# A graph layer's edge pass on one core: its last 13 quads written out per engine, and two gathers of padding left out

## What is computed

```python
k, q, v = (typed_linear(x, ntype, W).reshape(n, H, HD) for W in (Wk, Wq, Wv))
kw = typed_linear_heads(k[src], etype, att)
a = jnp.sum(kw * q[dst], axis=-1) * pri[:, etype].T / np.float32(np.sqrt(HD))
amax = jax.ops.segment_max(a, dst, num_segments=n)
ae = jnp.exp(a - amax[dst])
w = ae / jax.ops.segment_sum(ae, dst, num_segments=n)[dst]
m = typed_linear_heads(v[src], etype, msg) * w[:, :, None]
h = jax.ops.segment_sum(m, dst, num_segments=n).reshape(n, D)
h = typed_linear(h, ntype, Wa)
return h * alpha + x * (1 - alpha)      # alpha = sigmoid(skip)[ntype]
```

## Time and profile before

| | |
|---|---|
| median of 3 runs | 6516.59 us |
| the profiled execution | 6516.66 us |
| its span in the profile | 6514.9 us |
| PE busy | 4628.8 us (71%) |
| DVE busy | 4972.8 us (76%) |
| ACT busy | 4070.1 us (62%) |
| POOL busy | 4223.8 us (65%) |
| longest line of POOL (L563) | 3965.9 us in 4095 gathers |

### The profile page before, as it was taken

The page is one execution under the profiler, slowest core; times in us unless marked ns, Lnnn a source line. Parts: engine busy times, 40 slices in busy tenths (PEclk is TensorE's granted clock), DMA queues, the critical chain, the costliest instruction groups (busy, mean ns, idle before and its releaser), DMA issues.

```text
span 6514.9 us, 170550 instructions
## 1 busy us (share of the span) xinstructions
PE 4628.8 (71%) x33358; PEld 3951.0 (61%) x33359; DVE 4972.8 (76%) x14638; ACT 4070.1 (62%) x10772; POOL 4223.8 (65%) x4629
## 2 busy tenths in 40 slices
PE   7766666696666666976666679766666786666665
PEld 6665555575565555765655567655665676555553
DVE  6777777787777777777777777777777778777776
ACT  3467666645666665456666654666666547666665
POOL 1577777526777774277777743777777347777773
PEclk9888888798888888988888879788888898888887
DMA  6433333353333333533333335333333353333331
GB/s 223 140 108 107 107 107 108 91 235 104 107 107 107 107 107 101 230 99 107 107 107 107 107 120 210 100 107 106 107 107 106 139 191 102 107 107 106 106 108 54
DMA packets 306187, 783.84 MB, mean 120 GB/s; under 512 B 105775, under 2 KB 138900, under 8 KB 305012
## 3 DMA queue, kind: packets, MB, share of 16 engines
q0 software_dynamic: 196560, 537.00, 28.8%
q1 hardware_dynamic: 109092, 241.62, 9.9%
HBM read 573.87 MB, written 195.88 MB: 118 GB/s over the span
## 4 chain that ended last, share of the span: by engine, by line
PE 29%; DVEq 21%; issue 18%; DVE 17%; POOL 7%; DMA 4%; ACT 2%; ACTq 1%; POOLq 0%; SPq 0%
POOL rows L563 7%; DVEq L1446 7%; DVEq L1436 6%; PE ps L701 5%; PE ps L879 4%; PE ps L863 4%; DMA rows<-table,idx_now 3%; PE ps L884 3%; PE ps L725 3%; DVEq L286 3%; PE ps L712 3%; PE ps L695 2%; DVE prod L1430 2%; PE ps L878 1%; DVE wmsg L1408 1%
## 5 line engine op out<-in xcount | busy, mean ns | idle before, releaser
L563 POOL DMA_INDIRECT rows<-table,idx_now x4095 | 3965.9, 968 | 1389.4 <-issue 1145.7
L998 ACT ACTIVATE prod<-iota_n,dloc 128x128 bf16<-128x128 f32 x6240 | 1983.6, 389 | 21.0 <-issue 1.8
L878 PE MATMUL ps<-zeros,identb 128*128 128x132 bf16 x2080 | 516.5, 248 | 1517.8 <-DVE wmsg L1408 1248.1
L863 PE MATMUL ps<-qn,ohT 128*128 x8320 | 1429.9, 325 | 81.3 <-issue 61.7
L863 PEld LDWEIGHTS ps<-qn,ohT 128*128 128x128 f32 x8320 | 1252.1, 230 | 161.6 <-issue 143.1
L878 PEld LDWEIGHTS ps<-zeros,identb 128*128 128x128 bf16 x2080 | 225.1, 108 | 1690.6 <-issue 1571.4
L1003 ACT ACTIVATE ohf<-prod,ones 128x512 f32<-128x512 bf16 x1040 | 750.7, 722 | 731.4 <-PE ps L884 652.2
L879 PE MATMUL ps<-wmsg,ohf 128*128 128x132 f32 x4160 | 1122.8, 359 | 0.0
L1404 DVE TENSOR_TENSOR wmsg<-rows,weight 128x512 f32<-128x512 f32 x1040 | 724.1, 696 | 341.0 <-issue 309.4
L884 PE MATMUL ps<-wmsg,ohf 128*128 128x132 f32 x4160 | 976.2, 323 | 0.0
L1430 DVE TENSOR_TENSOR prod<-ps,rows 128x512 f32<-128x512 f32 x1040 | 716.5, 689 | 270.8 <-DMA rows<-table,idx_now 134.7
(11 more groups left out here) (166 smaller groups left out, 5474.2 us busy)
## 6 DMA issues: line engine op xcount, KB each, us to landing
table<-rows SPq DMA_DIRECT2D x245, 768.0 KB, 3.3
stage<-table SPq DMA_DIRECT2D x8320, 1.0 KB
rows<-table,idx_now POOLq DMA_INDIRECT x4095
rows<-in_node_type SPq DMA_DIRECT2D x5, 2613.0 KB, 10.5
rows<-stage SPq DMA_DIRECT2D x65, 128.0 KB
rows<-in_node_type SPq DMA_DIRECT2D x5, 512.0 KB, 4.2
out<-h SPq DMA_DIRECT2D x3, 704.0 KB
idx_row<-row_of SPq DMA_DIRECT2D x65, 0.5 KB
```

The lines of the kernel that those rows point to most:

```text
L563: pool.indirect_dma_start(out=rows[:, slot, j, :], out_offset=None, in_=table, in_offset=bass.IndirectOffsetOnAxis(ap=idx_now[:, half, c:c ...
L863: last = pe.matmul(ps[:, 2 + b, j * P:(j + 1) * P], ohT[:, b, j, :], qn[:, at(ts[j]), :].rearrange("p a c -> p (a c)"), start=True, stop=True)
L878: pe.matmul(bank[:, AW:2 * AW], identb[:], zeros[:], start=True, stop=True)
L998: act.activation(squares[:, turn % 2, j * P:(j + 1) * P], iota_n[:], ACT.Square, bias=dloc[:, at(4 * q + j)], scale=-1.0)
```

## The change

It does four things:

1. **No padding gathers.** In slot 15 SP's rows are now those of step 0 and POOL gathers steps 1 to 3. In quad 207 POOL gathers step 1 alone (step 829), and the two padding steps keep old rows of the ring; their edges are masked as before. DVE's wait counts follow (`LAST_PLACE`, `landed`). That is 2 gathers less per layer, 4085 in all.
2. **The tail is a function of its own on PE, ACT and DVE**, called behind `positions`, which ends at quad 207. REST = 196 is the first quad that the tail sums, FINAL = 25 the last block.
3. **On PE** each of the first three pieces stands ahead of the sum that it stood behind, and piece 3 stands right behind piece 2, ahead of the sums of quads 198 and 199.
4. **On DVE** the add of quad 195 moves from ahead of piece 0 to behind it, the add of 196 from ahead of piece 1 to behind it, and the weigh of 198 and the add of 197 from ahead of piece 2 to behind it. ACT's order is unchanged.

```diff
+LAST_PLACE = 48 * (QUADS // 16 - 1) + 16 * (STEPS - 4 * (QUADS - 1) - 1)
...
-            for q in range(QUADS - RING, QUADS + LAG + 1):
+            for q in range(QUADS - RING, QUADS):
...
-                sp.dma_start(rows[:, RING - 1, 3, :], stage[:]).then_inc(s_side, 16)
+                sp.dma_start(rows[:, RING - 1, 0, :], stage[:]).then_inc(s_side, 16)
...
-                    for j in range(3 if slot == RING - 1 else 4):
+                    for j in (range(1, STEPS - 4 * (QUADS - 1)) if is_last(q, QUADS) else
+                              range(1, 4) if slot == RING - 1 else range(4)):
...
-                        ta = tiles_of(a, mybir.EngineType.PE)
...
-                        ...
...
+                        sum_group(a, b)
...
+                def tail():
+
+                    softmax_piece(0, FINAL, FINAL % 2)
+                    sum_group(REST, 0)
+                    softmax_piece(1, FINAL, FINAL % 2)
+                    sum_group(REST + 1, 1)
+                    softmax_piece(2, FINAL, FINAL % 2)
+                    softmax_piece(3, FINAL, FINAL % 2)
+                    for a in range(REST + 2, QUADS):
+                        sum_group(a, a % 2)
+
+                def sum_group(a, b):
+                    ta = tiles_of(a, mybir.EngineType.PE)
...
+                    ...
...
+                tail()
...
+                def exponents(m):
+                    act.wait_ge(s_smd, l * (SM * BLOCKS) + SM * m + 3)
+                    act.activation(fade4[:, 1, :], fade4[:, 0, :], ACT.Exp)
+                    act.activation(aT[:], aT[:], ACT.Exp).then_inc(s_sme, 1)
...
+                def tail():
+                    for a in range(REST + 1, QUADS):
+                        onehot(ohf, a, a % 2, a, l * QUADS + a - 1).then_inc(s_ohf, 1)
+                        if a == REST + 3:
+                            exponents(FINAL)
...
-                              idx[:].rearrange("p (n s) -> p n s", s=2 * BS)[:, :, 2 * BS - 1:2 * BS],
+                              idx[:].rearrange("p (n s) -> p n s", s=2 * BS)[:, :, 2 * BS - 4:2 * BS - 3],
...
-                            dve.wait_ge(s_gath[slot], (l * (QUADS // RING) + use) * 48 + 48)
+                            landed = 16 * (STEPS - 4 * (QUADS - 1) - 1) if is_last(q, QUADS) else 48
+                            dve.wait_ge(s_gath[slot], l * LAST_PLACE + use * 48 + landed)
...
+                def weigh(a):
+                    slot, b = a % RING, a % 2
+                    w = weight[:, slot // BQ, (slot % BQ) * 4 * H:(slot % BQ + 1) * 4 * H].rearrange(
+                        "p (s h) -> p s h", h=H)
+                    dve.wait_ge(s_agg, l * QUADS + a - 1)
+                    dve.tensor_tensor(
+                        wmsg[:, b, :, 0:D].rearrange("p s (h c) -> p s h c", h=H),
+                        rows[:, slot, :, D:ROW].rearrange("p s (h c) -> p s h c", h=H),
+                        w.rearrange("p s (h c) -> p s h c", c=1).broadcast_to((P, 4, H, HD)), ALU.mult)
+                    dve.tensor_copy(wmsg[:, b, :, D:AW], w).then_inc(s_wm, 1)
+
+                def add(c):
+                    ts = tiles_of(c, mybir.EngineType.DVE)
+                    dve.wait_ge(s_agg, l * QUADS + c + 1)
+                    for i in range(2):
+                        window = acc_[:, at(ts[2 * i], 2), :].rearrange("p a c -> p (a c)")
+                        last = dve.tensor_tensor(window, window, ps[:, 4 + 2 * (c % 2) + i, 0:2 * AW], ALU.add)
+                        if i == 0:
+                            dve.drain()
+                    dve.drain().then_inc(s_add, 1)
+
+                def tail():
+                    par = FINAL % 2
+                    weigh(REST)
+                    softmax_piece(0, FINAL, par)
+                    weigh(REST + 1)
+                    add(REST - 1)
+                    softmax_piece(1, FINAL, par)
+                    add(REST)
+                    softmax_piece(2, FINAL, par)
+                    weigh(REST + 2)
+                    add(REST + 1)
+                    softmax_piece(3, FINAL, par)
+                    for a in range(REST + 3, QUADS):
+                        weigh(a)
+                        add(a - 1)
+                        if a == QUADS - BQ:
+                            fade_sums(a)
+                    add(QUADS - 1)
                 queries(l)
                 positions(dve, body)
+                tail()
```

More of the change, by code:

```diff
@@ L342, in gnn @@
         SM = 4
+        REST = QUADS - LAG
+        FINAL = BLOCKS - 1
         raw_dst = flat[:, 8192:8192 + CB * P]
@@ L890, in body @@
                         softmax_piece(k, m, 1 - slot // BQ)
+                def tail():
[9 more added lines that the diff above has]
+                    ta = tiles_of(a, mybir.EngineType.PE)
+                    pe.wait_ge(s_ohf, l * QUADS + a + 1)
+                    pe.wait_ge(s_wm, l * QUADS + a + 1)
+                    if not is_first(a, 2):
+                        pe.wait_ge(s_add, l * QUADS + a - 1)
+                    for i in range(2):
+                        bank = ps[:, 4 + 2 * b + i, :]
+                        pe.matmul(bank[:, AW:2 * AW], identb[:], zeros[:], start=True, stop=True)
+                        pe.matmul(bank[:, 0:AW], ohf[:, b, 2 * i, :], wmsg[:, b, 2 * i, :],
+                                  start=False, stop=True, skip_group_check=True)
+                        on = nc.s_assert_within(
+                            ta[2 * i + 1] - ta[2 * i], 0, 1,
+                            skip_runtime_bounds_check_because="a step moves on by one tile at most")
+                        last = pe.matmul(bank[:, at(on * AW, AW)],
+                                         ohf[:, b, 2 * i + 1, :], wmsg[:, b, 2 * i + 1, :],
+                                         start=False, stop=True, skip_group_check=True)
+                    last.then_inc(s_agg, 1)
                 queries(l)
                 positions(pe, body)
+                tail()
             layers(pe, edges_, output_, project_, between_)
@@ L1018, in body @@
                     if k == 3:
-                        act.wait_ge(s_smd, l * (SM * BLOCKS) + SM * m + 3)
-                        act.activation(fade4[:, 1, :], fade4[:, 0, :], ACT.Exp)
-                        act.activation(aT[:], aT[:], ACT.Exp).then_inc(s_sme, 1)
+                        exponents(m)
                     if b == 0 and not beyond(q + 2):
@@ L1460, in body, with fade_sums @@
                         keep_part(l, n)
+                def fade_sums(a):
+                    t0 = tiles_of(a, mybir.EngineType.DVE)[0]
+                    msgs = acc[:, at(t0), 0:D].rearrange("p a (h c) -> p (a h) c", h=H)
+                    exps = acc[:, at(t0), D:AW].rearrange("p a h -> p (a h)")
+                    dve.tensor_tensor(msgs, msgs, fade[:].rearrange("p (h c) -> p h c", c=1
+                                                                   ).broadcast_to((P, H, HD)), ALU.mult)
+                    dve.tensor_tensor(exps, exps, fade[:], ALU.mult)
+                    dve.drain()
```

8 lines of the change are left out of this document (1 added, 7 removed).

## The result

| | this kernel | before |
|---|---|---|
| median, us | 6473.76 (6472.45 to 6474.86, 4 runs) | 6518.88 (6512.33 to 6522.35, 4 runs) |
| ratio, 95% interval | 0.9932 (0.9915 to 0.9949) | |
| profiled execution, us | 6472.45, span 6470.6 | 6516.66, span 6514.9 |

The change saves 45.1 us by the medians and 44.2 by the profiled executions. The forecast was 6474.

The account below looks back on a forecast made before the run. POOL's gathers were taken to pace the edge phase, and engines waiting for each other in turn the tail. Gains of 6.1 + 23.6 + 12.8 = 42.5 us off 6516.66 gave 6474.2, forecast 6474, range 6464 to about 6493.

Parts of the forecast that it names:

- Gathers: Layers 1 to 4, quad 207: last gather starts 2.50 us earlier, so DVE's wait before `prod` goes; gain 6.1 us.
- Order of the tail: Layers 1 to 4, weigh of 196 to 201: 8.08 us of waits go, some 2.2 come; 4 x 5.9 = 23.6 us.
- The single waits: New DVE waits in the tail: add of 196 0.5, piece 2 0.4, piece 3 0.1, adds of 198 and 199 0.7, 0.5.
- the rest 15.4, unchanged: From the weigh of 201 to the last add's end, order is the old one and its 15.4 us stay.
- the upper bound, 6.5 us a layer: Tail gain per layer if PE's clock rises one sum or more earlier, adding about 0.6 us to 5.9.
- Layer 5: Layer 5: `prod` of 207 gains 5.5 us, and with POOL's adds meeting later operations the weigh of 201 gains 12.8.
- the adds hold up six DVE operations: Layer 5, piece 3 to weigh of 201: six all-SBUF DVE operations each wait for one POOL add, about 8.7 us lost.
- The sum: All layers: 6.1 + 23.6 + 12.8 = 42.5 us gained, from 6516.66 to 6474.2.
- the load still catches the gather of 829: Rival, layer 5: the residual's load delays the last gather, gain 5.0 instead of 12.8, time 6482; chance 0.15.
- the bound in the sense of that rival: Rival, tail: PE's clock stays at 0.50 to the end, each layer gains 4.3, time 6482; chance 0.09.
- The landings under the weight loads: Rival, quad 207: `prod` waited for landings under SP's weight loads, not gathers; gain 28.6, time 6488; chance 0.06.
- The jumps of the loop: Rival, loop turns: each of 55 jumps, 2.98 us now, gets 1.0 us dearer, time 6529; chance 0.03.

Follow-up runs that it names:

- the late load: The kernel with the new tail order but the old gathers, SP loading layer 5's residual only after quad 207's scores are done; 6490.74 us, one run.
- the first run: The changed kernel with its new gathers but PE and DVE in the old tail order; 6503.61 us, ratio 0.998 to the kernel before.

## Why the prediction was right

- **Gathers, forecast 6.1 us, measured 6.9.** The mechanism is as described; one gather away nearly suffices. The term was a little small in each layer: I left 0.1 us of issue ahead of `prod`, and there is none (3.22 us from one `prod` to the next in three layers).
- **Order of the tail, forecast 23.6 us, measured 25.8.** Up to the weigh of 201 I had 18.0 us and the layers show 18.00 to 18.23. The single waits are those forecast: 0.60, 0.35, 0.19, 0.47 and 0.26 against 0.5, 0.4, 0.1, 0.7 and 0.5. The step that was too small is "the rest 15.4, unchanged": it is 14.3 in three layers, since the clock rose before the weigh of 201 and stayed up. (Layer 2 had 14.8 before, so it gains only 0.5 by that.) I had kept this for the upper bound, 6.5 us a layer, and layers 1 and 4 passed it with 6.8 and 6.9. Layer 3 kept its 15.1: its clock rose ahead of the weigh of 201 too, but fell back behind it. That the clock is the whole of the 1.1 us is read from these stretches, not tested by a run.
- **Layer 5, forecast 12.8 us, measured 13.1.** 5.7 for the gather ahead of the load, where the forecast had 5.5, and 7.9 up to the weigh of 201, less 0.5 behind it. That the adds hold up six DVE operations was right to the number. The price was 8.7 us up to the weigh of 201, and the run without the adds has 7.5 there; its 8.9 us for the whole tail are near the 8.7 by chance, since 1.4 of them lie behind the weigh of 201, where the forecast had nothing.
- **The sum.** 42.5 forecast, 45.8 measured in these places, and 1.5 given back in the rest of the span, where I had nothing. So the forecast was some 2 us short of the 44.2 saved between the profiled executions. That the median came to lie 0.4 us beside the forecast's 6474.2 is luck in part: the sum started from 6516.66, and the median of the kernel before is now 6518.88.

The rivals. That the load still catches the gather of 829 did not come: `prod` of quad 207 has no idle time in layer 5. Its mechanism is real, though, as the late load showed. These lines of layer 5 (POOL's last gather, SP's load) show how far apart the two now are:

```profile
6336.34 0.96 POOL L567 DMA_INDIRECT rows<-table,idx_now  x1 [0.30 <-issue]
...
6339.75 0.85 SPq L486 DMA_DIRECT2D qn<-in_x  x1
```

The gather starts 3.41 us ahead of the load, where the forecast had 2.40. With one padding gather kept 1.16 us were enough for a wait of 0.35; with both kept the lead was 0.08 us and the wait 5.04. The Trainium skill (DMA: Bandwidth & Descriptors, Queues, rings and completion order) has the rule for it, that a semaphore's write lands behind every earlier write of its DMA engine; the runs agree with it, but none separates it from slower landing of the rows themselves. PE was not the bound in the sense of that rival, as its clock rose earlier instead of not at all; but it is so close to DVE now, and ACT with it, that 0.4 us taken from DVE gains nothing. The landings under the weight loads were ruled out by the first run, where the gathers alone took the wait away in layers 2 to 5. The jumps of the loop are unchanged: 3.09 us at the turn that had 2.98, and 2.75 to 3.09 at the ten turns of layer 1, where the kernel before has 2.75 to 3.07.

```profile
1020.12 3.09 issue
```

## What to carry to other kernels

Where two engines hand work to each other in turn, put on the producer's queue first what the other waits for, and what only adds up results behind it; then write the same order on both, since here DVE alone in the old order brought a wait of its own back (3.12 us, a net 1.6 up to quad 201). Work that is only padding can still be the last thing that lands: what it costs is read from when the last of it starts, not from its share of the engine. Before making an engine finish sooner, look for the barrier behind it and for who else arrives there, with the time from its last work to its arrival counted in.

## What I had not expected

- POOL needs 8.3 us from the end of its last add to the barrier (8.30 and 8.31 in two kernels). It was covered in this kernel and in the one before.
- Splitting POOL's add is not free: 14.8, 16.6, 19.8 and 24.4 us for 6, 12, 24 and 48 pieces, 0.2 to 0.3 us for each piece more. With 12 pieces DVE's tail gains nothing (41.91 us against 42.09), with 24 it gains 3.1.
- How much a small copy can lose: one of 16 columns with a single SBUF input, which the prediction had counted among the six, goes from 0.17 us to 2.31 under adds of 2.47 us, and to 0.42 under adds of 0.51.
- In layer 1 PE's granted clock rose ahead of the weigh of quad 201 and not behind it, with the same matmuls standing closer together (6.41 of 7.00 us busy in the stretch before the rise). An order that was chosen to shorten waits seems also to have brought back part of the clock, though in layer 3 it fell once more.
